# A Mamba, mixture-of-experts and sliding-window attention kernel on one core: a new order of the units of a turn

## The reference, cut to what matters

```
proj = hidden @ in_proj_w.T; hs, gate = proj[..., :256], proj[..., 256:]
u = silu(conv(hs) + conv_b)                        # depthwise, 4 taps
x_dbl = u @ x_proj_w.T                             # 64 + 16 + 16 columns
dt, Bm, Cm = rmsnorm of each of the three parts
dt = softplus(dt @ dt_proj_w.T + dt_proj_b)
h_t = exp(dt*A) * h_(t-1) + (dt*u) * Bm            # 256 channels x 16 states
y = (sum over the 16 states of h*Cm + u*D) * silu(gate); out = y @ out_proj_w.T

mixture of experts: each token goes through one of 8 experts (128-512-128), by argmax
attention: 16 heads of width 8, band of +-32 tokens, softmax, output projection
feed-forward: gate, up and down products with dequantised weights (128-384-128), silu
```

## Time and profile before

| | |
|---|---|
| time, median of 3 runs | 1077.52 us (1076.68 to 1078.6) |
| the profiled execution | 1082.89 us, its span 1081.1 us |
| busy: PE, DVE, ACT, POOL | 831.0, 803.9, 644.6, 414.6 us |
| chain that ended last | DVE 31%, PE 26%, issue 21%, POOL 11%, ACT 7% |
| granted TensorE clock, mean | 0.88 |

### The profile page before, as it was taken

How to read it: one execution, slowest core, us unless ns; L and a number is a source line. 1 busy time by engine, 2 the same in 40 slices (tenths; PEclk the granted TensorE clock), 3 DMA queues, 4 the chain that set the end, 5 groups by cost and what they waited for, 6 DMA issues and landing times.

```text
span 1081.1 us, 15591 instructions
## 1 busy us (share of the span) xinstructions
PE 831.0 (77%) x5226; PEld 572.8 (53%) x5226; DVE 803.9 (74%) x1059; ACT 644.6 (60%) x1985; POOL 414.6 (38%) x241
## 2 busy tenths in 40 slices
PE   1935778885877797879787978797879787888775
PEld 0713767773644574457445744574457445644443
DVE  7566344466888878887888788878887889777475
ACT  0232546572668457845784578556855685578564
POOL 2167122115453246324722473247315632553000
PEclk9857899997999799989998989789978896899897
...
GB/s 234 134 169 104 244 239 278 272 230 90 113 90 64 84 125 101 75 76 123 100 87 66 114 102 99 65 116 98 100 64 112 96 98 71 152 107 25 21 11 11
DMA packets 85951, 123.19 MB, mean 114 GB/s; under 512 B 8560, under 2 KB 43760, under 8 KB 85744
## 3 DMA queue, kind: packets, MB, share of 16 engines
...
...
## 4 chain that ended last, share of the span: by engine, by line
DVE 31%; PE 26%; issue 21%; POOL 11%; ACT 7%; DMA 2%; SPq 0%; DVEq 0%; POOLq 0%
DVE hst L801 11%; POOL hc L1194 6%; DVE dBu L793 4%; POOL x_res L1178 3%; PE work L1306 3%; PE y_bank L1287 2%; ACT dA L1016 2%; DVE nmax L946 2%; PE more L1419 2%; PE work L1465 2%; DVE dc L863 2%; ACT pexp L1092 1%; DVE fsg L955 1%; DVE dw L857 1%; PE work L1332 1%
## 5 line engine op out<-in xcount | busy, mean ns | idle before, releaser
L1194 POOL TENSOR_TENSOR hc<-hst,bcr 128x1024 f32<-128x1024 f32 x116 | 277.3, 2390 | 504.5 <-DVE dBu L793 498.7
L801 DVE TENSOR_TENSOR_SCAN hst<-dA,dBu 128x1024 f32<-128x1024 f32 x128 | 291.7, 2279 | 34.8 <-ACT dA L1016 28.2
L1287 PE MATMUL y_bank<-pk,hc 128*128 128x128 f32 x1024 | 159.5, 305 | 84.2 <-POOL hc L1194 68.0
L1287 PEld LDWEIGHTS y_bank<-pk,hc 128*128 128x128 f32 x1024 | 130.7, 157 | 110.1 <-POOL hc L1194 80.1
L793 DVE TENSOR_TENSOR dBu<-dtu,bcr 128x1024 f32<-128x1024 f32 x128 | 176.5, 1379 | 15.8 <-DMA bcr<-bc_d 2.6
L1016 ACT ACTIVATE dA<-dt,neg_a 128x511 f32<-128x511 f32 x256 | 171.1, 729 | 12.7 <-DVE hst L801 10.2
L1419 PE MATMUL more<-pk,pexp 128*96 128x128 f32 x480 | 101.1, 309 | 37.4 <-ACT pexp L1092 32.1
L1105 ACT COPY pT<-more 96x512 f32<-96x512 f32 x120 | 69.9, 582 | 64.6 <-PE more L1419 64.3
L1419 PEld LDWEIGHTS more<-pk,pexp 128*96 128x96 f32 x480 | 60.4, 136 | 72.1 <-issue 51.4
L1092 ACT ACTIVATE pexp<-work,nmax 128x96 f32<-128x96 f32 x240 | 78.3, 342 | 22.9 <-DVE nmax L946 22.4
L1092 ACT ACTIVATE pexp<-work_l,nmax 128x96 f32<-128x96 f32 x240 | 78.0, 338 | 4.0 <-DVE nmax L946 3.6
...
## 6 DMA issues: line engine op xcount, KB each, us to landing
bcr<-bc_d SPq DMA_DIRECT2D x128, 512.0 KB
...
```

Of the source, the lines that this page charges most:

```text
L801: v.tensor_tensor_scan(hst[n % 2][:].rearrange("p h t -> p (h t)"), dA[n % 2][:].rearrange("p h t -> p (h t)"), dBu[:].rearrange("p h t -> ...
L1194: g_.tensor_tensor(hc[n % 2][:], hst[n % 2][:], bcr[n % RING][:, 1:2, :].to_broadcast([P, NH, L]), ALU.mult).then_inc(s_hc, 1)
L1287: last = t.matmul(y_bank[h][:, q], hc[n % 2][:, h, q], ident, is_transpose=True, start=False, stop=(n == N - 1 and j == NT - 1))
```

## The change

The tables become lists of single units with an explicit place in the slot: `HEAD` (before everything else of the slot), `MID` (between the scan of a step and its product), and `REST`. The unit `step` is split: `step` is the scan alone, `product` is `dBu` of the next step and POOL's `hc`. `sum` of step m stands two slots behind step m (`SUM_LAG`). The start of `y_bank` is a unit of its own (`init`), and hs0 stands behind `init` and `out`. The tanh of hs0 and hs1 are units th0 and th1. zg0, zg1 move behind xdbl. The feed-forward is split into `fg`, `fs`, `fu`, `fh`, and its products use `bank0` (index 5) instead of two of the three banks, behind dtp1. The four indirect transfers are single units in slots 5, 7, 9 and 11.

```diff
-FFN_AT = {12: 0, 17: 1, 21: 2}
-PRE_AT = {0: ['xnT', 'hs0'], 2: ['u0'], 3: ['hs1'], 4: ['zg0', 'u1'], 6: ['sg0', 'zg1'], 7: ['sg1'], 9: ['xdbl'], 10: ['ss'], 12: ['xdr'], 13: ['bc'], 16: ['dtT'], 18: ['dtp0'], 19: ['drl0', 'dtp1'], 21: ['drl1'], 22: ['de'], 23: ['dw'], 24: ['dln'], 25: ['dt'], 26: ['dtu'], 27: ['start']}
+STEP_AT = (0, 1, 3, 4, 6, 8, 10, 12, 14, 16, 17, 19, 21, 22, 24, 26)
+EDGE = [("attn", "y_end"), ("finish", "rdT"), ("pre", "xnT"), ("attn", "gated"), ("attn", "yT"), ("scan", "init"), ("attn", "out"), ("pre", "hs0")]
+HEAD = {11: [("pre", "sg0", 0)], 12: [("pre", "sg1", 0)], 15: [("pre", "drl0", 0)], 16: [("pre", "drl1", 0)],
+        18: [("attn", "fs", 0)], 19: [("attn", "fh", 0)], 20: [("attn", "fs", 1)], 21: [("attn", "fh", 1)],
+        22: [("attn", "fs", 2)], 23: [("attn", "fh", 2)]}
+MID = {3: [("scan", "slots", 0)], 8: [("pre", "ss", 0)], 19: [("pre", "dw", 0)], 24: [("pre", "dt", 0)], 26: [("pre", "dtu", 0)]}
+REST = {1: [("attn", "x1", 0)],
+        2: [("attn", "ln_a", 0), ("pre", "th0", 0), ("pre", "u0", 0)],
+        3: [("attn", "ln_b", 0), ("pre", "hs1", 0)],
+        4: [("pre", "th1", 0), ("pre", "u1", 0), ("attn", "q", 0), ("attn", "k", 0)],
+        5: [("attn", "v0", 0), ("attn", "v1", 0), ("finish", "avg", 0), ("scan", "rows", 0)],
+        6: [("attn", "v2", 0)],
+        7: [("finish", "fin", 0), ("finish", "attnT", 0), ("attn", "v3", 0), ("pre", "xdbl", 0), ("scan", "rows", 1)],
+        8: [("finish", "y_out", 0)],
+        9: [("pre", "xdr", 0), ("pre", "bc", 0), ("scan", "rows", 2)],
+        10: [("pre", "zg0", 0)], 11: [("pre", "zg1", 0), ("scan", "rows", 3)],
+        13: [("pre", "dtT", 0)], 14: [("pre", "dtp0", 0)], 15: [("pre", "dtp1", 0)],
+        17: [("pre", "de", 0), ("attn", "fg", 0)], 18: [("attn", "fu", 0)], 19: [("attn", "fg", 1)],
+        20: [("attn", "fu", 1)], 21: [("attn", "fg", 2)], 22: [("attn", "fu", 2)],
+        23: [("pre", "dln", 0)], 27: [("attn", "rden", 0), ("pre", "start", 0)]}
-STEP_AT = (0, 1, 3, 5, 7, 8, 10, 12, 14, 16, 17, 19, 21, 22, 24, 26)
+SUM_LAG = 2
...
+        units += HEAD.get(slot, [])
...
             units.append(("scan", "step", n))
+        units += MID.get(slot, [])
+        if n is not None:
+            units.append(("scan", "product", n))
         units += [(lane, "averages", g) for lane, g in of("values", slot)]
-        if n is not None:
-            units.append(("scan", "sum", n))
+        units += [("scan", "sum", m) for m in range(N - 1) if STEP_AT[m] + SUM_LAG == slot]
...
-           "oL": 0, **{f"gate{k}": GATE_BANK[k] for k in range(HC)}, **{f"up{k}": 2 for k in range(HC)}}
+           "oL": 0, **{f"gate{k}": 5 for k in range(HC)}, **{f"up{k}": 5 for k in range(HC)}}
...
         def take0(eng, b, key):
             before(eng, s_free0, b * L0_N + L0_USES.index(key))
+            at = BANK0.index(("pre", key))
+            lane, last = BANK0[at - 1]
+            a = b - LAG["attn"] + LAG["pre"] - (at == 0)
+            if lane == "attn" and 0 <= a < B:
+                done1(eng, a, FFN_KEY[last])
```

More of the change, by code:

```diff
@@ L184, in early @@
             put(0, slot, ("down", m - 1))
-    put(1, 0, ("clear", 0), ("rows", 0))
+    put(1, 0, ("clear", 0), ("slots", 0), *[("rows", j) for j in range(NT)])
     return at
@@ L227 @@
 L0_N = len(L0_USES)
+FFN_KEY = {f"{n}{k}": f"{key}{k}" for n, key in (("fg", "gate"), ("fu", "up")) for k in range(HC)}
 O_AT = RG * KW
```

119 lines of the change are left out of this document (61 added, 58 removed).

## The result

| | before | after |
|---|---|---|
| median, us | 1077.84 (4 runs, 1076.68 to 1078.60) | 1103.12 (4 runs, 1098.10 to 1106.19) |
| profiled execution, its span | 1082.89, 1081.1 | 1103.31, 1101.5 |
| mean granted clock | 0.882 | 0.879 |
| scan step 0 of turn 0 at | 79.7 | 80.6 |
| turn 0 | 163.6 | 167.0 |

The ratio is 1.022, interval 1.0185 to 1.0255, so the loss is clear of no change. I had forecast 1040 us, with a range to 1073. In the profiled executions turns 1 to 6 lose 3.3 us each, 20 us together. Turn 0 adds 3.3 and the lead 0.9, and turn 7 gives 3.0 back. That makes 21 us and not the 25 of the medians, because the profiled execution of before lies 5 us above its median.

The account below looks back on a forecast made before the run. No single engine was taken as the bound; the order of the queues decides. Six turns -36, turn 0 +3 and turn 7 -4 gave -37 us, so 1040 us on the median's terms, range 1016 to 1073 (likeliest case 1027 to 1055).

Parts of the forecast that it names:

- The walk of the first part: Step-by-step timing of a full turn from scan step 0 to scan step 7: 44.4 us, a gain of 0.6 us.
- The rows for `dBu` of step 4 land about +16.6 [...], just in time: First part of a turn: step 4's rows arrive 16.6 us after scan step 0, so `dBu` does not wait for them.
- The wait for the x_proj product: First part: xdbl ends at +31.6, `ss` starts at +32.1, and DVE stands 4.5 us with the scan behind it.
- Rival D: Slower through the wait for xdbl, break-even if it ends at +37.6; lower PE clock gives about 1116, half 1093; chance 0.06.
- From `ss` to scan 7: End of the first part: `ss` at +32.1, `rr` taking 2.27 us, second `sg` waiting some 1.9 us, scan 7 at +44.4.
- three long rows of before: `dBu` 4.30, `dw` 2.13, `dc` 2.67 us, each started beside a POOL product and read as held up by POOL.
- The second part: From scan step 7 to the turn's end: 51.2 us work plus 7.7 us idle, 58.9 us, a gain of 5.4.
- 5.95 us of blocking: Second part: POOL holds DVE up 3.07 + 1.44 + 1.44 us a turn, and all of it goes.
- the idle time, 7.7 us in the prediction: Second part: waits of the two `drl`, `fsg` 0, `fh` 0 and 1, and short gaps, changing from 6.5 us.
- rival C: Gain given back: the one-bank chain doubles new waits in the second part to 13 us, about 1072 us; chance 0.20.
- Turn 0 and turn 7: Turns outside the six full ones: turn 0 net +3 us (0 to +5), turn 7 -4 us (0 to -9).
- The signs: Wrong if the `xsq` wait passed 10 us, idle before `drl`, `fsg`, `fh` 13 us a turn, or `dBu` stayed long.

Follow-up runs that it names:

- Experiment 1: The changed kernel with SyncE's issue of the step 4 B and C rows moved in among the small transfers of own_heads: 1077.3 us, ratio to before 0.9974.
- experiment 2: The changed kernel with the x_proj product issued in slot 5 behind v1, instead of slot 7 behind v3: 1077.9 us, ratio to before 0.9993.
- experiment 12: The kernel before with only the softplus' dw, dc and its two last adds moved between scan step and product of slots 24 and 26: 1073.0 us, ratio 0.9950.
- Experiment 3: The changed kernel with sg1, drl1, fh0, fh1 and fs2 put behind the scan step of their slot instead of ahead: 1039.4 us, ratio to before 0.9616.
- 13: The kernel before with only the tanh of hs0 moved from ahead of step 1's decays to slot 2, ahead of u0: 1070.8 us, ratio 0.9935.
- 7: The kernel before with only the four indirect transfers put one each in slots 5, 7, 9, 11 instead of all in slot 10: 1075.8 us, ratio 0.9976.
- 10: The kernel before with only each sum two slots behind its step and the initial product as its own unit in slot 0: 1076.7 us, ratio 0.9976.
- the version without the three waits: The changed kernel with step 4's rows issued inside own_heads, x_proj in slot 5, and five units behind their scan: 995.0 us, ratio to before 0.9226.

## Why the prediction was wrong

**The walk of the first part** had the sum of the steps right and one date wrong. Its first steps hold: the wait for `dA` went, scan 1 came at +3.65 (I had it end at +6.0), `u` at +9.7 (start; I had its end at +11.0), scan 3 started at +14.0. The step that failed is "The rows for `dBu` of step 4 land about +16.6 [...], just in time". I took that landing from turn 7, where SyncE's queue is 3 us further; in the full turns of before these rows were issued only at +14.5, and it did not show, since VectorE took them up at +26.9 (496.47), behind two waits of which the change takes one away and puts the other behind this `dBu`. In after they came at +21.0. Experiment 1 shows the price, 25.9 us. With the rows on time the rest of my walk up to `ss` holds: there TensorE takes 13.0 us from the end of hs1 to the end of xdbl (I had 12.7), and `ss` waits 4.3 us (I had 4.5).

**The wait for the x_proj product** I had seen and named (4.5 us, `ss` at +32.1). It was 6.0 us, and `ss` came at +35.4. The second convolution came out better than I had it, 3.60 us at a granted clock of 1.00, so that hs1 ended at +16.9 instead of +18.9. But from there to the end of xdbl TensorE took 17.9 us instead of 12.7. The sum of step 3 stood 2.97 us for a product that was late through the rows, and the lower clock behind this wait cost some 1.8 us. So xdbl ended at +34.8 instead of +31.6. Experiment 1 shortens the wait by 1.8 us, experiment 2 removes it. Rival D (0.06) had this place, and 1103 us lies between its two prices, 1093 and 1116. Its cause, TensorE at the lower clock up to xdbl, held for 4.6 us only, behind the wait that the late rows made; in experiment 1 the granted clock stays at 1.00 up to the end of xdbl. Its point of break-even, +37.6, was wrong, as it relied on the gain of the second part.

**From `ss` to scan 7** I had 12.3 us and it took 14.8. Both `sg` wait (1.9 and 2.0) where I had one wait, and `rr` takes 3.21 us where I had 2.27. The second is what the Trainium skill says ("SBUF — State Buffer", "Who interferes with whom"), by which GpSimd waits for a two-input instruction of VectorE that holds the port, and which I cited but left out of the sum. The trace of after agrees: `rr` has a median of 3.21 us over 8 in after and 2.27 in before, and `dBu` starts 0.17 us ahead of it. One of the three long rows of before does not fall under the rule as I gave it: `dw` has one input and not two. That it too was held up is shown by its 0.67 us in experiment 12, where no POOL product runs beside it.

**The second part.** That the 5.95 us of blocking go was right: `dw` is at 0.7, `dc` at 1.2, every `dBu` of this part at 1.23 us, busy time 51.0 where I had 51.2. The term that was mis-sized is the idle time, 7.7 us in the prediction, 12.6 in the trace: 5.1 for the two `drl` (I had 3.6), 4.0 for the first two `fh` (2.6), 3.5 for the rest, where I had 1.5. This is rival C's size (13). Why each wait came out longer than I had it was not tested. What I did not do is ask what these waits are worth where they stand. Experiment 3 shows that five of them, all ahead of a scan that was ready, cost 8.6 us a turn. It also shows that the chain through one bank, C's reason, does not set the time: its units were taken up later, and the turn became shorter.

**The two parts together.** In this turn the first part misses my walk by 5.8 us (50.2 against 44.4) and the second by 4.6 (63.5 against 58.9). That is 10.4 us a turn and 62 us in six turns, which is the 63 us between the forecast and the measured time.

**The parts of the change one by one.** Of the four parts that I ran alone on the kernel before none did harm (experiment 12: 5.7 us, 13: 7.5, 7: 2, 10: 2). On the version without the three waits, the spread transfers are worth 32 us, the gates behind x_proj 39 (with x_proj's own place) and the lag of the sums nothing. The others were not taken back there. So the change held large gains that its own waits hid. With them it is 25 us slower than before, without them 83 us faster. My sum gave the transfers no more than an on-time product of step 8. What the feed-forward through bank 0 is worth by itself stays open, as it was not tried alone.

**Turn 0 and turn 7** were right: +3.3 (I had +3) and -3.0 (-4).

**The signs.** None of the signs by which I said I would know that I was wrong came: the wait for `xsq` was 6.0 us and not above 10, the idle time before `drl`, `fsg` and `fh` 10.4 us and not above 13, and no `dBu` above 2.4 us over the run. The rows of step 4 were not on that list.

The forecast was thus the sum of a right list of gains and a walk that stopped looking once a wait was removed. Parts of two rivals, a later xdbl ahead of `ss` and longer waits in the second part, happened in the same turn, and I had given no chance to the two together.
